# A gated cross-attention and mixture kernel: a ten-pass hardware loop written out as straight code, and the increments that only carried a wait taken out

## The reference, cut to what matters

```python
def reference(x, ctx_1024, g_xattn, g_ffn, Wk, Wq, Wv, sim_matrix, gates, q_proj, k_proj, v_proj, o_proj):
    # cross-attention, queries from layernorm(x), keys and values from the context
    x = x + tanh(g_xattn[0]) * xattn(ctx_1024, layernorm(x), Wk, Wq, Wv)
    # mixture: h = layernorm(x)
    logits = (h / |h|) @ (sim / |sim|) - sigmoid(gates)
    w = softmax(where(mask > 0, relu(logits), -inf))     # top 2 where no gate is open
    q = sum_e w_e * (h @ q_proj[e]);  k, v likewise
    o = softmax(q @ k.T / sqrt(128)) @ v
    return x + tanh(g_ffn[0]) * sum_e (w_e * o) @ o_proj[e]
```

## Time and profile before

| | |
|---|---|
| median of 3 runs | 880.05 us (879.66 to 880.3) |
| the profiled execution's own time | 878.19 us |
| its span, first to last instruction | 876.4 us |
| PE busy | 822.3 us, 94% |
| DVE, ACT, POOL busy | 71%, 59%, 63% |
| chain that ended last | PE 80%, DVE 6%, ACT 5%, issue 4%, POOL 2%, DMA 1% |

### The profile page before, as it was taken

One profiled execution on the slowest core, in us unless ns is written; L12 is line 12 of the kernel. 1 busy time (PEld: TensorE's weight loads), 2 busy tenths in 40 slices (PEclk: granted clock), 3 DMA queues, 4 the chain that ended last, 5 costly groups with the idle time before them and its releaser, 6 DMA issues.

```text
span 876.4 us, 16223 instructions
## 1 busy us (share of the span) xinstructions
PE 822.3 (94%) x4344; PEld 458.2 (52%) x4344; DVE 618.1 (71%) x1575; ACT 518.2 (59%) x1148; POOL 550.7 (63%) x588
## 2 busy tenths in 40 slices
PE   4579999999999999999999999999999999999974
PEld 3445555555555555555555555555555555545431
DVE  3777577777686867768686776868677686876545
ACT  3555657565665756566575656657575565656353
POOL 2265567576685857567585756759475765857464
PEclk9999999999999999999999999999999999999999
DMA  8753655453654645364564536465463636546342
GB/s 223 193 193 106 192 176 189 139 200 130 219 160 166 209 156 191 111 227 151 186 210 153 192 108 218 145 205 191 152 212 111 226 111 210 185 182 217 93 159 72
DMA packets 58531, 150.49 MB, mean 172 GB/s; under 512 B 5568, under 2 KB 22144, under 8 KB 58496
## 3 DMA queue, kind: packets, MB, share of 16 engines
q1 hardware_dynamic: 57776, 150.00, 51.8%
q10 hardware_dynamic: 720, 0.08, 0.1%
HBM read 145.34 MB, written 4.72 MB: 171 GB/s over the span
## 4 chain that ended last, share of the span: by engine, by line
PE 80%; DVE 6%; ACT 5%; issue 4%; POOL 2%; DMA 1%; ACTq 1%; DVEq 0%; POOLq 0%
PE acc_v L893 17%; PE acc_k L893 17%; PE acc_q L893 16%; PE acc_o L909 16%; DVE zo_full L756 2%; ACT pc L550 2%; PE m L1032 2%; PE m L960 2%; PE m L931 2%; POOL stage L460 2%; PE oT_p L985 2%; PE m L1014 1%; PE m L923 1%; PE m L1001 1%; DVE zq_full L746 1%
## 5 line engine op out<-in xcount | busy, mean ns | idle before, releaser
L455 POOL TENSOR_TENSOR zq<-zq_full,zq 128x512 f16<-128x512 f32 x192 | 224.6, 1171 | 201.0 <-ACT zq L508 200.9
L460 POOL TENSOR_TENSOR stage<-zo_full,stage 128x512 f16<-128x512 f32 x208 | 239.4, 1160 | 69.7 <-ACT stage L516 69.7
L508 ACT ACTIVATE zq<-zq_full 128x512 f16<-128x512 f32 x256 | 161.1, 630 | 203.6 <-DVE zq_full L746 199.2
L909 PE MATMUL acc_o<-stage,w_hi 128*128 128x512 f16 x512 | 193.5, 381 | 10.3 <-POOL stage L460 7.3
L746 DVE TENSOR_TENSOR zq_full<-wq_bc,x2T_p 128x512 f32<-128x512 f32 x256 | 172.9, 677 | 35.1 <-ACT x2T_p L609 26.5
L893 PE MATMUL acc_q<-zq,w_hi 128*128 128x512 f16 x512 | 194.7, 380 | 0.0
L893 PE MATMUL acc_k<-zq,w_hi 128*128 128x512 f16 x512 | 194.5, 380 | 0.0
L893 PE MATMUL acc_v<-zq,w_hi 128*128 128x512 f16 x512 | 194.5, 380 | 0.0
L756 DVE TENSOR_TENSOR zo_full<-stage,oT_p 128x512 f32<-128x512 f32 x256 | 169.9, 677 | 6.5 <-PE oT_p L985 5.9
L516 ACT ACTIVATE stage<-zo_full 128x512 f16<-128x512 f32 x256 | 158.2, 629 | 25.7 <-DVE zo_full L756 25.1
L909 PE MATMUL acc_o<-stage,w_lo 128*128 128x512 f16 x256 | 97.5, 381 | 0.0
(11 more groups left out here) (141 smaller groups left out, 1067.6 us busy)
## 6 DMA issues: line engine op xcount, KB each, us to landing
wq_bc<-w_rows SPq DMA_DIRECT2D x128, 512.0 KB, 5.0
stage<-w_rows SPq DMA_DIRECT2D x128, 512.0 KB, 4.0
out_dram<-x_all SPq DMA_DIRECT2D x16, 256.0 KB, 4.3
ctx_g<-in_ctx_dram SPq DMA_DIRECT2D x16, 154.0 KB
x_all<-in_x_dram SPq DMA_DIRECT2D x2, 256.0 KB, 6.7
x_all<-in_x_dram SPq DMA_DIRECT2D x1, 512.0 KB, 9.2
w_rows<-wT SPq DMA_DIRECT2D x16, 32.0 KB, 3.2
wq_sb<-in_L_xattn_Wq_dram SPq DMA_DIRECT2D x1, 64.0 KB, 5.5
```

The source lines that it names most:

```text
L455: nc.gpsimd.tensor_tensor(zq[:, 1, e % Z_SLOTS, :], zq_full[:, e % F_SLOTS, :], zq[:, 0, e % Z_SLOTS, :], ALU.subtract).then_inc(zq_lo_poo ...
L460: nc.gpsimd.tensor_tensor(zo[:, 1, e % Z_SLOTS, :], zo_full[:, e % F_SLOTS, :], zo[:, 0, e % Z_SLOTS, :], ALU.subtract).then_inc(zo_lo_poo ...
L508: nc.scalar.activation(zq[:, 0, e % Z_SLOTS, :], zq_full[:, e % F_SLOTS, :], ACT.Copy).then_inc(zq_hi_done, 1)
L909: last = nc.tensor.matmul(acc[O][:], w[:, O, e, :], zo[:, half, e % Z_SLOTS, :], start=(e == 0 and n == 0), stop=(e == E - 1 and n == 2))
```

## The change

Every pass is written out with constant counts. `passes` has one Python loop from -2 to 17. The hardware loop is gone from all five engines, and with it the branch, the counting instructions and the register arithmetic of the waits. On DVE the six waits on `x_in` ahead of the loop are gone; `first_stats` waits in each pass for the one load that it needs. The semaphore `passed` and all calls of `plain` are gone.

```diff
@@ -45,7 +45,6 @@
-    LOOP = (3, NG - 3)
@@ -258,24 +256,14 @@
-        def plain(eng):
-
-            eng.sem_inc(passed, 1)
-
...
-        def passes(eng, body, loads=()):
-            for i in range(-2, LOOP[0]):
-                body(i)
-            for load in loads:
-                eng.wait_ge(load, 16)
-            with eng.Fori(LOOP[0], LOOP[1]) as i:
-                body(i)
-            for i in range(LOOP[1], NG + 2):
+        def passes(eng, body):
+            for i in range(-2, NG + 2):
                 body(i)
@@ -353,7 +341,6 @@
                 wait(sp, w_rows_in, 16 * g + 16)
-                plain(sp)
@@ -419,9 +406,7 @@
                 wait(pool, bn1_done, 2 * g + 2)
-                plain(pool)
                 wait(pool, xn_done, g)
-                plain(pool)
@@ -619,12 +601,10 @@
             def stats(g, src, bn, mv, done):
-                plain(dve)
                 for b in range(G):
                     last = nc.vector.bn_stats(bn[:, b, :], rows(src, g, b))
                 last.then_inc(done, 1)
                 wait(dve, done, 2 * g + 1)
-                plain(dve)
@@ -859,7 +838,7 @@
-            passes(dve, body, x_in)
+            passes(dve, body)
```

More of the change, by code:

```diff
@@ L174, in flamingo_gated_moe_attention @@
         consts = sem("consts")
-        passed = sem("passed")
         tanh_done = sem("tanh_done")
```

## The result

| | before | after |
|---|---|---|
| median | 880.2 us (879.66 to 880.41, 6 runs) | 876.48 us (874.87 to 877.04, 6 runs) |
| ratio, 95% interval | | 0.9954 [0.9941, 0.9967] |
| profiled execution, its span | 878.19, 876.4 us | 876.63, 874.8 us |

The change makes the kernel 0.46% faster, 3.7 us, where 2.5 us (0.28%) were forecast. The interval reaches from 2.9 to 5.2 us. The direction and most steps were right; the gain was larger. The profiled execution of before was a short one, 2.0 us under its median; that of after lies 0.15 us above its own.

What follows compares the result with a forecast made beforehand. PE was taken to bound the kernel, busy 822.3 of 876.4 us. Loop waits 1.9 plus setup increments 0.6, all else zero, gave 2.5 us less than 880.05: forecast 877.6 us, range 876.4 to 879.6.

Steps and rivals of the forecast that it cites:

- The bound: In a full pass PE waits only at step 4's first logit product, for ACT's `x2T`; 5.7 us over ten loop passes.
- The setup's increments: Setup chain until 54 us: removing plain increments saves 0.4 us on DVE and 0.2 on POOL, sum 0.6 us.
- The waits in the loop: Wait before the logit product, passes 3 to 12: 0.20 us saved in nine, 0.08 in pass 3, 1.9 us together.
- Two links: Chain to the logit product: scores ready to DVE's maximum saves 0.08 us, low part to ACT's first exponential 0.08.
- The third: Same chain, DVE's maximum to its low part: 0.99 us in loop pass 12 against 0.95 in written-out pass 13.
- The plain increments in the passes: In `stats`, `gate_logits` and POOL's roots: none on the chain to the logit product, PE waits for no other; zero.
- Branch, counters and registers on PE, POOL and SP: Loop instructions outside the DVE and ACT chain: removing them gains zero, since PE's row of matmuls covers them.
- Longer code: Written-out instruction stream of PE, about 19 and 23 packets in 505 us: costed at zero.
- Rival 2: Instruction blocks arrive late on PE, making the kernel slower: 881.7 us; chance 0.06.
- 1: Only part comes: the chain settles as in pass 2 and setup gives little; 1.4 us less, 878.65; chance 0.22.
- 3: The branch was costly: nine back edges at 0.85 us each, 7.7 us, time 869.9; chance 0.01.
- 4: The change does nothing: waits served no sooner, another operand as late; time stays at 880.0; chance 0.07.

Runs made afterwards that it cites:

- e11: The changed kernel with one increment put back, the one between `bn_stats` and `bn_aggr`: 878.24 us, 0.9988 of the kernel before.
- e12: The changed kernel with all increments put back but the one between `bn_stats` and `bn_aggr`: 876.39 us, 0.9968 of the kernel before.
- e1: All passes written out as in the changed kernel, but every plain increment kept: 877.39 us, 0.9979 of the kernel before.
- e2: The kernel before, hardware loop kept on all engines, plain increments taken out of setup and written-out passes only: 879.91 us, ratio 1.0003.
- e8: The kernel before with 47 extra matmuls, their product unread, in PE's idle times of the last two passes: 876.9 us, ratio 0.9968.
- e3: The changed kernel with the hardware loop given back to PE, POOL and SP, increments inside it: 875.86 us, 0.9958 of the kernel before.

## Why the prediction was right and wrong

- **The bound.** Right. PE's one wait in a full pass is before the logit product, and everything that the change won after the setup passed through it or, in pass 0, through the waits for `x` and `ctxT`; I had named one short wait there, and the wait for `x` shows as idle time in the changed kernel's rows but not in those of before.
- **The setup's increments: 0.6 us.** Right, 0.64 measured. The split was less so: I gave four places on DVE 0.4 us, and e11 shows 0.32 for the increments between `bn_stats` and `bn_aggr`, e12 0.30 for all the others. The price per increment, 0.10 us on the sequencer, held also in the passes.
- **The waits in the loop: 1.9 us, bounds 1.2 to 2.8.** Too large. Before against e11, in which every pass settles, gives 506.07 - 504.80 = 1.27 us, near the low bound; before against e1, with passes 3 and 4 at 0.29, gives 1.61. Two links were forecast rightly, 0.08 + 0.08 us a pass, and measure 0.09 and 0.08. The third, maximum to low part, was to shrink by 0.04 as in pass 13, and with the increments in place it grows by 0.03 (0.99 to 1.02), since an earlier maximum waits longer for POOL. The term was mis-sized by taking pass 13 (0.37 us) for the settled state. e1 and e11 settle at 0.44, which pass 2 had shown as 0.45; pass 13 is the first after the loop, and its multiply takes 0.31 us, between the free and the held ones. That it had not settled is argued, not shown.
- **"The plain increments in the passes ... Zero, hidden by PE's matmuls."** This is the step that failed, and it is why the gain was larger than forecast. Their cost is 0.97 us in the ten loop passes (e11 against after) and 0.34 in passes 0 to 2 (e2 against before), 1.3 us. (In e8, the kernel before up to the tail, the 0.34 are 0.17.) The reason given, that none is on the chain from L960 to L923, was true of the links that the chain of waits shows. But the chain has a second entrance, DVE's multiply, which ends with POOL's low part, by the page because of a port that the two engines share, and no semaphore tells of it. The rows were there: the multiply of 128x4 numbers took 0.35 us in pass 12 and ended with POOL's low part.
- **Branch, counters and registers on PE, POOL and SP: zero.** Right: e3 has them all and is as fast as the changed kernel. The rule of the Trainium skill on taken branches (page "Runtime: NRT & Kernel Launch", section "Instruction fetch mechanics") holds where the target is outside the current window of two pages. Here nine back edges came with 2 and 4 packets in all, and none after 222 us; whether the loop's start lay inside that window no run shows.
- **Longer code: zero.** Right: 22 and 23 packets of the instruction queues from 187 to 692 us, where 2 and 4 were the earlier trace rows, and no idle time of PE put down to issue. Rival 2 falls.
- **The sum.** Measured by pieces: 1.27 + 0.97 + 0.34 + 0.64 + 0.02 = 3.24 us, against 2.5 forecast. Two errors of opposite sign: the loop's waits 0.6 too high, the increments 1.3 too low (0.3 and 1.0 if e1 is the kernel between). That the sum came as near as it did is luck in part. The medians say 3.7; the rest of 0.5 is inside the interval, and the tail alone varies by more.
- **Rivals.** 1 assumed pass 2's 0.45 for all passes, and was right on this for as long as the increments stand; they were taken out as well. 2 and 3 are refuted by the time and the rows, and 4 by idle times that did fall.
- **The chances.** Faster had 0.67 and came. The time, 876.48, lies on the lower edge of the range, 876.4; the gain of 3.72 us taken from the 880.05 on which the forecast stood gives 876.33, just below it. The lower bound held the largest price of each term that I had counted, and none for the one at zero.

## What to carry to other kernels

Before a wait or an increment is costed at zero because "nobody on the chain waits for it", look at what runs *beside* each link of the chain on the engine that shares a port with it. A tiny operation that takes longer than its size explains, and ends together with an operation of another engine, is such a link; compare its duration where the neighbour is absent. Where a written-out pass is taken as a model of what loop passes will become, take one that has others of its kind behind it, and undo the change one part at a time before adding up the terms: here the parts on two engines did not add. Before work is shared with an idle engine, look at what that engine makes for the others and in which order: DVE's idle time in the tail was the lead by which it fed ACT and POOL.

## What the hardware showed that I had not expected

- DVE's 128x4 multiply: 0.23 us free, 0.25 to 0.40 when POOL's low part outlasts it, ending 0.02 to 0.03 us behind it.
- DVE's 128x512 low part: 0.69 us alone, 1.15 beside one of POOL's.
- One semaphore increment on DVE's sequencer per pass, in the written-out kernel: 0.10 us of PE's time, through ACT and POOL, 1 us over ten passes.
- The loop on DVE alone 1.74 us, on ACT alone 1.81, on both 2.24; from scores ready to maximum it takes 0.23 us with the loop on DVE alone and 0.11 with it on both, for the same instructions on DVE.
- The same tail code in 42.35 us at a granted clock of 0.93 and in 43.97 at 0.84, and in 40.8 at 0.99 when idle PE is given matmuls to do: more work, 3.2 us less time (876.35 to 873.19 in medians).
